# A graph network on one core: the second attention's sums split otherwise between VectorE and TensorE, scatter targets copied by ScalarE, and two runs of 48 gathers limited to four in flight

## The chip, the core and the metric

The kernel runs on one core of one Trainium2 chip. It is written in Bass: each engine (TensorE or PE, VectorE or DVE, ScalarE or ACT, GpSimd or POOL, and SyncE or SP, which issues transfers) runs its own instruction stream, and semaphores are the only order between them. The metric is the device time of one execution in microseconds (us). The kernel before took 3353.75 us, the median of three runs (3352.17 to 3357.39).

## What is computed

A graph of 1250 nodes (768 numbers each) and 20000 edges, sorted by destination, goes through a pre-norm GATv2 block of two attentions (8 heads, then 1 head) and a relational graph encoder with 34 relations and one GCN step. The second attention is what the change is about; in it `heads` is 1 and each edge needs

```
fs = x @ Ws + bs;  fd = x @ Wd + bd
e = leaky_relu(fs[src] + fd[dst], 0.2)        # one row of 768 per edge
logits = sum(e * attn)
m = segment_max(logits, dst)
ex = exp(logits - m[dst]);  denom = segment_sum(ex, dst)
out = segment_sum(ex / denom[dst] * fs[src], dst)
```

The leaky ReLU is split as 0.2·s + 0.8·max(s, 0); the first part is linear and comes ready in column 768 of the projected rows, so the edge work is one add (fs + fd), one `max(·,0)·attn` with a sum along the row, and a weighted sum of rows.

## The kernel before

**Chunks.** The edges are cut into groups of S = 4 edges of one destination; 128 groups, one on each partition, are a chunk. A record (`rec`) names each group's four source rows, its destination, and where its partial sum goes. There are 44 chunks, as 11 turns of a loop over U = 4 buffer slots.

**The stage `attention_single`.** For each chunk:

- SP loads the record (L961), three chunks ahead, once the old record of that slot has been read; one of the reads it waits for is the copy of the scatter target (`to_ok`).
- POOL, two chunks ahead of the arithmetic (`gather_rows`), issues one indirect gather of the destination's `fd` row (`own`, L893) and four of the `fs` rows (`row`, L889), 128 rows of 776 numbers each. Then it issues the scatter of an older chunk's sums (`second_d<-sum`, L942) and copies the scatter target of the chunk out of its record (`to<-rec`, L933), so that the record's slot can be loaded anew.
- DVE adds `own` to rows 0, 1 and 2 (L1392, three instructions, both inputs in SBUF). PE forms the sum of row 3 in PSUM: identity × row, then identity × own, in two halves of 384 columns (L1345 and L1347). DVE then makes four dot products (L1405): `max(sum,0)·attr` with an accumulated sum, for rows 0 to 2 with both tensors in SBUF, for row 3 with the sum in PSUM. Small instructions follow: softmax arguments (L1414 to L1419), relation counts (L1428, L1432), the running denominator (L1440, L1442).
- ACT takes the exponentials (L1325), makes five diagonal matrices of the weights (L1329) and later copies the chunk's sum out of PSUM (L1317). PE multiplies the diagonals with the four rows (L1360) and with the running sum (L1365).

DVE's order in one turn is: arguments of chunk n, counts of n, sums and dots of n+1, denominator of n. PE's order is: pS of n+1, then the products of n.

**Two runs of gathers elsewhere.** In the first stage, which sorts the edges and projects the rows, POOL issues 48 gathers (EARLY) of edge groups one behind the other (L510), then 20 marks; a mark (L222) waits for the mark four before it. In the stage between attention and relations it issues 48 gathers of count rows (L1817). In both runs all gathers raise one semaphore, which is waited for once, at its full count.

## Time and profile before

| | us |
|---|---|
| median of 3 runs | 3353.75 |
| the profiled execution | 3372.56 |
| its span, first to last instruction | 3371.1 |
| PE busy | 2760.3 |
| DVE busy | 2187.0 |
| POOL busy | 1722.6 |
| ACT busy | 1617.7 |

Only 1.5 us of the profiled execution lie outside its span. A share of busy time says little here, because the stages have different limits: the second attention lasts about 410 us of the span, and the long product of the relations (L2263) over 1000.

### The profile page before, as it was taken

Reading aid. Unit: us, or ns where it says so; the run is one execution under the profiler, and the core shown is the slowest. Engines: PE = TensorE matmul, PEld = TensorE weight load, DVE = VectorE, ACT = ScalarE, POOL = GpSimd, SP = SyncE. Lnnn points to the kernel's source line nnn. Section 1 sums busy time; section 2 is a strip of 40 time slices with the busy share of each in tenths; the row PEclk is TensorE's granted clock in tenths of the full one; section 3 lists DMA queues with packets and bytes.
Section 4 is the critical chain, followed back from the end, with each engine's and each line's share of the span. In section 5 each row is a group of like instructions: output and inputs, shape, how many; then the busy total and the mean of one; then the engine's idle time right before and its main releaser. Section 6 shows DMA issues by size and latency. Waiting matters only on the chain. (4 is left out here: it accounts for less than half of the span.)

```text
span 3371.1 us, 53614 instructions
## 1 busy us (share of the span) xinstructions
PE 2760.3 (82%) x11962; PEld 2042.9 (61%) x11985; DVE 2187.0 (65%) x3989; ACT 1617.7 (48%) x5047; POOL 1722.6 (51%) x2089
## 2 busy tenths in 40 slices
PE   5637789888689799995377999999999976676599
PEld 3314445454345455552247999999999973333499
DVE  6503789989666689884365666566566646767554
ACT  0000799999622133331344655656665556767100
POOL 3660556556477588883503444444444436767200
PEclk9859899999889899996698999999999998888799
DMA  4212546555442577775228777777777756667412
GB/s 141 84 18 91 175 151 182 168 170 174 155 120 81 168 230 227 233 231 186 66 91 267 231 245 240 235 237 243 232 244 237 239 129 213 211 218 221 151 62 85
DMA packets 212101, 596.86 MB, mean 177 GB/s; under 512 B 75813, under 2 KB 78905, under 8 KB 211871
## 3 DMA queue, kind: packets, MB, share of 16 engines
q0 software_dynamic: 96256, 380.68, 36.2%
q1 hardware_dynamic: 93487, 163.45, 15.6%
q10 hardware_dynamic: 22304, 52.11, 4.9%
q8 instruction: 22, 0.36, 0.0%
q14 instruction: 32, 0.26, 0.0%
HBM read 491.85 MB, written 161.57 MB: 194 GB/s over the span
## 5 line engine op out<-in xcount | busy, mean ns | idle before, releaser
L2263 PE MATMUL pO<-wh,gT 128*128 128x384 f32 x3264 | 867.9, 340 | 20.8 <-ACT gT L2214 8.3
L2263 PEld LDWEIGHTS pO<-wh,gT 128*128 128x128 f32 x3264 | 593.4, 188 | 26.6 <-issue 13.8
L2263 PE MATMUL pO<-wl,gT 128*128 128x384 f32 x1632 | 546.6, 335 | 0.0
L889 POOL DMA_INDIRECT row<-fs_d,rec x368 | 436.6, 1186 | 113.7 <-issue 112.5
L2279 DVE TENSOR_SCALAR cut<-pT 128x768 int32<-128x768 int32 x137 | 131.0, 956 | 373.1 <-ACT gT L2214 197.2
L1090 ACT ACTIVATE sj<-sj 128x96 f32<-128x96 f32 x1080 | 287.6, 268 | 62.1 <-DVE sj L1202 57.2
L178 PE MATMUL pO<-wt,hT 128*128 128x384 f32 (+1 forms) x720 | 254.6, 512 | 65.8 <-issue 31.4
L2263 PEld LDWEIGHTS pO<-wl,gT 128*128 128x128 f32 x1632 | 307.9, 189 | 0.0
L2214 ACT ACTIVATE gT<-cut 128x256 fp32r<-128x256 f32 x822 | 291.9, 410 | 28.1 <-DVE cut L2282 4.3
L2413 PE MATMUL pR<-row,share 128*128 128x384 f32 x352 | 148.7, 574 | 121.0 <-DMA row<-y_d,rec 39.5
L178 PEld LDWEIGHTS pO<-wt,hT 128*128 128x128 f32 (+1 forms) x720 | 141.9, 199 | 172.9 <-issue 89.8
L889 POOL DMA_INDIRECT row<-y_d,rec x184 | 195.4, 1062 | 92.5 <-issue 47.1
L1128 PE MATMUL pS<-row,ident 128*128 128x384 f32 x368 | 162.7, 525 | 96.1 <-DVE sj L1202 67.0
L222 POOL DMA_INDIRECT marked_d<-marks,recc x160 | 205.6, 1285 | 64.7 <-issue 49.9
L1360 PE MATMUL pA<-row,share 128*128 128x384 f32 x704 | 234.4, 486 | 0.1
L1149 PE MATMUL pA<-row,ident 128*128 128x384 f32 x704 | 234.2, 486 | 0.0
L178 PE MATMUL pO<-settle_wt,hT 128*128 128x384 f32 x480 | 172.4, 519 | 70.2 <-ACT hT L1880 49.8
L2139 POOL DMA_INDIRECT g<-hr_d,gindex x138 | 159.2, 1153 | 126.7 <-POOL keys L2136 74.5
L1090 ACT ACTIVATION_READ_ACCUMULATOR sj<-sj 128x1 f32 x1080 | 202.1, 187 | 8.0 <-issue 8.0
L2203 ACT ACTIVATE sign<-startrow,after 128x1279 bf16<-128x1279 f16 (+1 forms) x139 | 188.4, 1355 | 27.5 <-DMA startrow<-seen_d 26.4
L2292 DVE TENSOR_TENSOR wl<-raw,wh 128x768 fp32r<-128x768 f32 x204 | 195.5, 959 | 7.0
L2133 POOL TENSOR_SCALAR sourcef<-total 128x1 f32<-128x1 f32 x138 | 30.6, 221 | 322.6 <-ACT sign L2203 320.2
(388 smaller groups left out, 5626.6 us busy)
## 6 DMA issues: line engine op xcount, KB each, us to landing
raw<-in_L_gnn_W_rel_dram SPq DMA_DIRECT2D x204, 384.0 KB
startrow<-seen_d ACTq DMA_DIRECT2D x141, 320.0 KB
fs_d<-of SPq DMA_DIRECT2D x18, 388.0 KB
fd_d<-of SPq DMA_DIRECT2D x18, 388.0 KB
row<-fs_d,rec POOLq DMA_INDIRECT x368
ha<-first_d SPq DMA_DIRECT2D x10, 384.0 KB
ha<-second_d SPq DMA_DIRECT2D x10, 384.0 KB
kept_d<-y SPq DMA_DIRECT2D x10, 384.0 KB
```

The lines of the kernel that those rows point to most:

```text
L178: last = pe.matmul(dst[0:rows, q, 0:HALF], rows_t[:, c * P:c * P + rows], w[:, c, lo:up], start=c == 0, stop=c == KC - 1)
L222: pool.indirect_dma_start(marked_d[k], bass.IndirectOffsetOnAxis(ap=keys, axis=0), marks[0:EP], None)\
L889: pool.indirect_dma_start(b["row"][u][:, j, :].bitcast(words), None, table, bass.IndirectOffsetOnAxis(ap=b["rec"][u][:, 2 * j + field:2 * ...
L1090: last = act.activation(of_head, of_head, ACT.Copy, accum_out=dots[off % U][:, j, h:h + 1])
L1128: pe.matmul(pS[j][:, q, 0:HALF], ident[:], row[off % U][:, S // 2 + j, lo:up], start=True, stop=False)
L1149: last = pe.matmul(pA[:, q, 0:HALF], ident[:], row[u][:, j, lo:up], start=j == 0, stop=j == S - 1)
L1360: last = pe.matmul(pA[u % 2][:, q, 0:HALF], share[u % 2][:, 1 + j, :], row[u][:, j, lo:up], start=j == 0, stop=False)
L2139: pool.indirect_dma_start(g[:, b, :], None, hr_d, bass.IndirectOffsetOnAxis(ap=gindex[b][:], axis=0))\
L2203: act.activation(sign[:, 0:COUNT[b]], seen_row[b][:, 0:COUNT[b]], ACT.Sign, bias=half, scale=-1.0, accum_out=total[b][:]).then_inc(total_o ...
L2214: act.activation(gT[:, c].bitcast(F32R), cut[:, :, c * P:(c + 1) * P], ACT.Copy).then_inc(gT_ok.sem, 1)
L2263: last = pe.matmul(pO[:, q, 0:HALF], gT[:, c, half, :].bitcast(F32R), w[:, c, lo:up].bitcast(F32R), start=c == 0 and k == 0, stop=c == KC ...
L2292: dve.tensor_tensor(wl[b][:, c, :].bitcast(F32R), raw[b * KC + c], wh[b][:, c, :], ALU.subtract).then_inc(w_ok.sem, 1)
```

## The change

```
+OPEN = 4
 # first stage, the 48 gathers of L510 (the 48 of L1817 likewise, with crow_in)
+            edges_in2 = sems(st, *[f"edges_in2_{k}" for k in range(OPEN)])
                     for g in range(EARLY):
+                        if g >= OPEN:
+                            pool.wait_ge(edges_in2[g % OPEN], 16 * (g // OPEN))
                         pool.indirect_dma_start(early[:, g, 0:S * 2], None, table_rows, bass.IndirectOffsetOnAxis(
-                            ap=early[:, g, R_ROW:R_ROW + 1], axis=0)).then_inc(edges_in2, 16)
+                            ap=early[:, g, R_ROW:R_ROW + 1], axis=0)).then_inc(edges_in2[g % OPEN], 16)
 # scatter targets: POOL's keep_target is left out in the second attention, ACT does
+        def target_by_act(act, b, i, off):
+            u = off % U
+            rec_wait(act, b, i, off)
+            sum_free(act, b, i, off)
+            act.activation(b["to"][u][:], word(b, u, R_OUT), ACT.Copy).then_inc(b["to_ok"][u], 1)
 # attention_single
+                pW = pb("pW", [P, 2, 512], F32, st)
-                sum_ok = Signal(st, "sum_ok", BY_PE, U, U)
+                sum_ok = Signal(st, "sum_ok", 2, U, U)
                                 keep(i, u - 1)
+                                target_by_act(act, b, i, u)
 # PE
-                            for q, lo, up in HB:
-                                pe.matmul(pS[:, q, 0:HALF], ident[:], row[off % U][:, BY_PE, lo:up],
-                                          start=True, stop=False)
-                                last = pe.matmul(pS[:, q, 0:HALF], ident[:], own[off % U][:, lo:up],
-                                                 start=False, stop=True)
-                            last.then_inc(sum_pe.sem, 1)
+                            pe.matmul(pS[:, 0, 0:HALF], ident[:], row[off % U][:, BY_PE, 0:HALF], start=True, stop=False)
+                            pe.matmul(pS[:, 0, 0:HALF], ident[:], own[off % U][:, 0:HALF], start=False, stop=True)\
+                              .then_inc(sum_pe.sem, 1)
 # DVE
+                        v.mark(dve.tensor_copy(halves(pW), split(attr[:])))
-                            for j in range(BY_PE):
-                                logits.wait(dve, i, off - 1, j + 1)
-                                dve.tensor_tensor(leak[:, j, :], row[off % U][:, j, 0:D], fd[:, 0:D], ALU.add)\
-                                   .then_inc(sum_ok.sem, 1)
+                            logits.wait(dve, i, off - 1)
+                            dve.tensor_tensor(leak[:, 0:BY_PE, :], row[off % U][:, 0:BY_PE, 0:D], over(fd[:, 0:D], 1, [P, BY_PE, D]),
+                                              ALU.add).then_inc(sum_ok.sem, 1)
+                            dve.tensor_tensor(pS[:, 1, 0:HALF], row[off % U][:, BY_PE, HALF:D], fd[:, HALF:D], ALU.add)\
+                               .then_inc(sum_ok.sem, 1)
-                                    ins = dict(out=split(leak[:, j, :]), in0=split(leak[:, j, :]), in1=split(attr[:]))
+                                    ins = dict(out=split(leak[:, j, :]), in0=split(leak[:, j, :]), in1=halves(pW))
```

Five things, then: one DVE instruction of 3 × 768 columns in place of three of 768; row 3's sum half by DVE (SBUF inputs, PSUM output) and half by PE; the attention vector for rows 0 to 2 read from a copy in PSUM (`pW`); the target copy on ACT behind its copy of the sums; and at most four gathers in flight in the two runs of 48.

How DVE's instructions stand in one slot of the loop, from the sums of a chunk to its last dot product. `leak` holds the sums in SBUF, `pS` is the PSUM tile of row 3, `attr` the attention vector in SBUF. Before:

```order
L1392 TENSOR_TENSOR leak<-row_2,own_2 128x768
L239 REGISTER_ALU
L1392 TENSOR_TENSOR leak<-row_2,own_2 128x768
L239 REGISTER_ALU
L1392 TENSOR_TENSOR leak<-row_2,own_2 128x768
L1395 TENSOR_TENSOR lin_2<-row_2,own_2 128x4
L239 ISA
L1405 SCALAR_TENSOR_TENSOR leak,dots_2<-leak,attr 128x768
```

And after (`pW` is the copy of the vector in PSUM):

```order
L1404 TENSOR_TENSOR leak<-row_2,own_2 128x2304
L1406 TENSOR_TENSOR pS<-row_2,own_2 128x384
L1409 TENSOR_TENSOR lin_2<-row_2,own_2 128x4
L240 ISA
L1419 SCALAR_TENSOR_TENSOR leak,dots_2<-leak,pW 128x768 x3
L240 REGISTER_ALU x2
L1419 SCALAR_TENSOR_TENSOR leak,dots_2<-pS,attr 128x768
```

Three adds became one of three times the length, a half-length add that writes PSUM follows it, and three of the four dot products read their second tensor from PSUM. Nothing else changes place on DVE.

How POOL's instructions stand in one slot of the same loop. Before:

```order
L889 DMA row_2<-fs_d,rec_2 128x776 x4
L942 DMA second_d<-sum_2,to_2 2560x912
L933 COPY to_2<-rec_2 128x1
L910 REGISTER_ALU
L239 REGISTER_ALU
L893 DMA own_2<-fd_d,rec_2 128x776
```

And after:

```order
L894 DMA row_2<-fs_d,rec_2 128x776 x4
L954 DMA second_d<-sum_2,to_2 2560x912
L915 REGISTER_ALU
L240 REGISTER_ALU
L898 DMA own_2<-fd_d,rec_2 128x776
```

The copy between the scatter and the next chunk's gathers is gone; the six transfers stay as they were.

## Rows read from the trace of the kernel before

**Rows 1.** Busy time in steady state of the second attention; then a page line, section 5.

```profile
core 0: us, PE busy (x) PEld busy (x) DVE busy (x) ACT busy (x) POOL busy (x), PEclk, DMA share, GB/s
1200.00:1500.00 300.00, 299.60 (x928) 175.60 (x927) 267.32 (x692) 93.52 (x238) 244.55 (x231) 1.00 0.78 231
...
L1360 PE MATMUL pA<-row,share 128*128 128x384 f32 x704 | 234.4, 486 | 0.1
```

**Rows 2.** Groups of instructions, 1200 to 1500 us: busy, mean ns | idle before, releasers.

```profile
L889 POOL DMA_INDIRECT row<-fs_d,rec x132 | 169.9, 1287 | 40.3 <-issue 39.4 <-DMA rec<-groups_d 0.9
L1405 DVE SCALAR_TENSOR_TENSOR leak<-leak,attr 128x768 f32<-128x768 f32 x99 | 89.5, 953 | 0.0
L1392 DVE TENSOR_TENSOR leak<-row,own 128x768 f32<-128x768 f32 x99 | 89.1, 955 | 16.7 <-DMA row<-fs_d,rec 9.3 <-issue 7.3
L1345 PE MATMUL pS<-row,ident 128*128 128x384 f32 x133 | 54.2, 488 | 0.4 <-issue 0.3
L942 POOL DMA_INDIRECT second_d<-sum,to x33 | 35.2, 1067 | 10.1 <-issue 10.1
L893 POOL DMA_INDIRECT own<-fd_d,rec x33 | 32.8, 994 | 5.1 <-issue 5.1
L1405 DVE SCALAR_TENSOR_TENSOR leak<-pS,attr 128x768 f32<-128x768 f32 x33 | 31.5, 954 | 0.6 <-DMA by_dst_d<-recs 0.6
L933 POOL COPY to<-rec 128x1 int32<-128x1 int32 x33 | 7.2, 218 | 0.0
```

**Rows 3.** Waits, 1200 to 1500 us: us in total, times, longest.

```profile
POOL row L889 <- issue: 39.4, 129, 0.3
DVE leak L1392 <- DMA row<-fs_d,rec: 9.3, 14, 1.2
```

**Rows 4.** Timeline of POOL and DVE, 1300 to 1340 us: start, us, instruction, idle before.

```profile
1305.68 2.70 DVE L1392 TENSOR_TENSOR leak<-row,own 128x768 f32<-128x768 f32 x3 [0.83 <-issue]
1305.97 1.48 POOL L889 DMA_INDIRECT row<-fs_d,rec  x1 [0.30 <-issue]
...
1309.50 1.52 POOL L889 DMA_INDIRECT row<-fs_d,rec  x1 [0.30 <-issue]
...
1315.32 2.70 DVE L1392 TENSOR_TENSOR leak<-row,own 128x768 f32<-128x768 f32 x3 [1.19 <-DMA row<-fs_d,rec]
...
1324.29 2.70 DVE L1392 TENSOR_TENSOR leak<-row,own 128x768 f32<-128x768 f32 x3
...
1328.11 1.51 POOL L889 DMA_INDIRECT row<-fs_d,rec  x1 [0.30 <-issue]
...
1333.32 2.69 DVE L1392 TENSOR_TENSOR leak<-row,own 128x768 f32<-128x768 f32 x3 [0.58 <-DMA row<-fs_d,rec]
```

**Rows 5.** Timeline of DVE and POOL in the first stage, 49.5 to 54 us.

```profile
49.84 2.82 DVE L721 TENSOR_TENSOR_SCAN startrow<-keyrow 128x1280 f32<-128x1280 f32 x1
50.77 2.88 POOL L222 DMA_INDIRECT marked_d<-marks,recc  x1 [0.30 <-issue]
52.70 1.49 DVE L722 TENSOR_TENSOR startrow<-startrow,keyrow 128x1280 f32<-128x1280 f32 x1
```

**Rows 6.** Timeline of DVE and POOL where DVE's second tensor is in PSUM.

```profile
2813.15 1.54 DVE L2473 SCALAR_TENSOR_TENSOR sum<-sum,rec,pC 128x1280 int16<-128x1280 int16 x1
...
2813.36 0.94 POOL L889 DMA_INDIRECT row<-y_d,rec  x1 [0.31 <-DVE sum L2468]
```

**Rows 7.** POOL's short transfers by line: duration ns min/median/max, first and last start.

```profile
L222 POOL DMA_INDIRECT marked_d<-marks,recc x160: 1170/1187/2884, 33.2 to 1096.3; - x160
L510 POOL DMA_INDIRECT early<-by_dst_d,early x48: 940/944/1042, 151.6 to 210.4; - x48
L1817 POOL DMA_INDIRECT crow<-rcnt_d,crec x48: 942/946/1680, 1592.4 to 1652.4; - x48
```

**Rows 8.** Two marks in a row; then busy time in two stretches, columns as in rows 1.

```profile
229.96 1.18 POOL L222 DMA_INDIRECT marked_d<-marks,recc  x1 [0.30 <-issue]
231.44 1.18 POOL L222 DMA_INDIRECT marked_d<-marks,recc  x1 [0.30 <-DMA marked_d<-marks,recc]
...
195.00:245.00 50.00, 10.70 (x17) 3.87 (x16) 0.00 (x0) 0.00 (x0) 37.09 (x37) 0.53 0.08 2
1617.00:1655.00 38.00, 0.00 (x0) 0.00 (x0) 0.00 (x0) 0.00 (x0) 28.16 (x31) 0.55 0.13 14
```

More of the change, by code:

```diff
@@ L292, in gnn_kernel @@
             rest_edge = sb("rest_edge", [P, S * 2], I32, st)
-            early_in, edges_in2, masked, edges_out, rest_in, rest_step, rest_out = sems(
-                st, "early_in", "edges_in2", "masked", "edges_out", "rest_in", "rest_step", "rest_out")
+            edges_in2 = sems(st, *[f"edges_in2_{k}" for k in range(OPEN)])
+            early_in, masked, edges_out, rest_in, rest_step, rest_out = sems(
+                st, "early_in", "masked", "edges_out", "rest_in", "rest_step", "rest_out")
             p_index = pb("p_index", [P, 2, 512], F32, st)
@@ L860, in _ @@
                     dve.wait_ge(masked, 1)
-                    dve.wait_ge(edges_in2, 16 * EARLY)
+                    for landed in edges_in2:
+                        dve.wait_ge(landed, 16 * (EARLY // OPEN))
                     dve.tensor_tensor(edges, edges, is_edge[:], ALU.mult).then_inc(masked, 1)
@@ L965, in load_records, with gather_rows @@
                 sp.sem_inc(b["sp_posted"], 1)
-        def gather_rows(pool, b, table, field, own, out_table, readers, done, words=F32):
+        def gather_rows(pool, b, table, field, own, out_table, readers, done, words=F32, targets=True):
             open_sums(pool, b)
@@ L987, in gather_rows @@
                     sums_out(pool, b, i, u - LAG, out_table, done)
-                    keep_target(pool, b, i, u)
+                    if targets:
+                        keep_target(pool, b, i, u)
             for k in range(LAG, 0, -1):
@@ L1304, in _ @@
                     def _(pool):
-                        gather_rows(pool, b, fs_d[0:1 + N], 0, fd_d, second_d, (summed,), (kept, den_ok, counted))
+                        gather_rows(pool, b, fs_d[0:1 + N], 0, fd_d, second_d, (summed,), (kept, den_ok, counted), targets=False)
                     @block.scalar
@@ L1398, in dot @@
                                 if j < BY_PE:
-                                    sum_ok.wait(dve, i, off, j + 1)
-                                    ins = dict(out=split(leak[:, j, :]), in0=split(leak[:, j, :]), in1=split(attr[:]))
+                                    sum_ok.wait(dve, i, off, 1)
+                                    ins = dict(out=split(leak[:, j, :]), in0=split(leak[:, j, :]), in1=halves(pW))
                                 else:
-                                    logits.wait(dve, i, off - 1, j + 1)
+                                    sum_ok.wait(dve, i, off)
                                     sum_pe.wait(dve, i, off)
@@ L1737, in settle_last @@
                     st, "den_in", "rden_ok", "cnt_in", "rcnt_ok", "rcnt_out", "rec_in")
-                crow_in, pool_step, rest_step, rest_out, rest_in = sems(
-                    st, "crow_in", "pool_step", "rest_step", "rest_out", "rest_in")
+                crow_in = sems(st, *[f"crow_in{k}" for k in range(OPEN)])
+                pool_step, rest_step, rest_out, rest_in = sems(
+                    st, "pool_step", "rest_step", "rest_out", "rest_in")
                 rel_const, present_in, summed, joined, seen_ok, seen_out, ntiles_ok, ends_ok, behind_ok, tile_ok = sems(
@@ L1816, in _ @@
                         for g in range(EARLY):
+                            if g >= OPEN:
+                                pool.wait_ge(crow_in[g % OPEN], 16 * (g // OPEN))
                             pool.indirect_dma_start(crow[:, g, :], None, rcnt_d, bass.IndirectOffsetOnAxis(
-                                ap=crec[:, g, R_NODE:R_NODE + 1], axis=0)).then_inc(crow_in, 16)
+                                ap=crec[:, g, R_NODE:R_NODE + 1], axis=0)).then_inc(crow_in[g % OPEN], 16)
                         more = pool.value_load(ctl[0:1, C_REST:C_REST + 1], min_val=1, max_val=MAX_TURNS * U)
@@ L1852, in _ @@
                         pool.sem_inc(posted, 1)
-                        pool.wait_ge(crow_in, 16 * EARLY)
+                        for landed in crow_in:
+                            pool.wait_ge(landed, 16 * (EARLY // OPEN))
                     @block.scalar
```

## The prediction, made before the changed kernel was run

> **What bounds the kernel now.** I first read the busy time of the second attention in steady state [rows 1]. In 300 us PE has 299.6 us of busy time: it looks like the bound. The matmuls are 928, and L942, which comes once a chunk, is there 33 times [rows 2]: 28 matmuls and 9.09 us a chunk, a pitch of 0.323 us, with nothing left. The stage has 704 / 16 = 44 chunks [rows 1].
>
> Then I read the groups of POOL in the same stretch [rows 2]. POOL's busy share is only 244.55 of 300 us, but busy plus the idle time in front of its instructions is 169.9 + 40.3 for the gathers of rows, 35.2 + 10.1 for the scatter, 32.8 + 5.1 for `own` and 7.2 for the copy: 300.6 us. The waits [rows 3] show that the idle part is 129 pauses, none over 0.3 us, put down to "issue": the fixed pause in front of each indirect transfer, not a wait for anybody. So POOL never waits for the other engines, and its stream sets 9.11 us a chunk. DVE, on the other hand, waited 14 times for the rows to land. PE and POOL are both full; DVE is third. From one first add to the next it needs 1333.32 − 1324.29 − 0.58 of waiting = 8.45 us [rows 4].
>
> Last, why POOL's gathers take 1287 ns on average when the 48 alike in the first stage take 944 [rows 2, 7]. In the timeline [rows 4] the gather at 1305.97 takes 1.48 us. It began inside the first of three DVE adds, which ended at 1305.68 + 0.955 = 1306.63, and it ended 0.82 us after that. The mark at 50.77 began inside one DVE scan of 2.82 us and took 2.88 us where the median mark takes 1.187 [rows 5, 7]; it outlasted the scan by 0.99 us. The reading: an indirect transfer that is issued while DVE runs an instruction with two SBUF tensors stands still until that one instruction ends. Where DVE's second tensor is in PSUM, a gather that starts inside DVE's 1.54 us takes 0.94, no stall at all [rows 6].
>
> For this the Trainium skill (SBUF — State Buffer, section "Who interferes with whom") has a rule: a DVE instruction with two SBUF inputs contends with a GpSimd one that reads SBUF, and the pair of ports is held for the whole instruction. The rows agree on GpSimd's side; the reverse, DVE held up by GpSimd, is not seen in them.
>
> **The change part by part.** All sums are in time of the profiled execution (3372.56 us), 19 us above the median of the runs; I add the difference to the median, 3353.75.
>
> PE. Two of four passes each of L1345 and of L1347 go. L1345 is there 133 / 33 = 4 times a chunk and L1347 as often, so 28 matmuls become 24: 24 × 0.323 = 7.76 us a chunk, 1.3 less. PE alone would give 44 × 1.3 = 57 us. This is collected only down to the next full engine.
>
> DVE. One add is 0.955 us [rows 2]; 1280 columns take 1.49 [rows 5], so a column costs (1.49 − 0.955) / 512 = 1.045 ns. The add of 2304 columns is then 0.955 + 1536 × 1.045 ns = 2.56 us, the one of 384 columns 0.55. Adds in a row overlap by about 0.08 us (three take 2.70, not 2.87 [rows 4]). Before: 3 × 0.875 = 2.63 to the next instruction. After: 2.48 + 0.47 = 2.95. DVE's floor becomes 8.45 + 0.32 = 8.77 us. Dots with the vector in PSUM: 954 ns with one PSUM tensor against 953 with none [rows 2], so no change. That the half add writes PSUM is not in the trace; between 0.47 and, if it cost as much as a whole add, 0.87 us, I take 0.47. The 0.4 more would put DVE at 9.2, which is no more than POOL takes below.
>
> POOL. Four things. (a) The copy goes, 0.22 us, but `own` then has the full pause of 0.30 in front of it in place of 5.1 / 33 = 0.155: net 0.07. (b) The stalls of now, 4 × (1.287 − 0.944) = 1.37 us a chunk, go: those in the dots because their vector is now in PSUM, those in the adds because there are no three short ones. POOL without stalls: 9.11 − 0.07 − 1.37 = 7.67. (c) One new stall comes. The long add runs 2.56 us. POOL starts something every 1.25 us (0.944 + 0.30), so some issue must fall inside it. If it starts s after the add, it ends 0.82 us after the add's end instead of 0.944 after its own start: a stall of 2.56 − s − 0.125 = 2.43 − s us, with s between 0 and 1.25. (d) Where s lies: POOL's last gather of a chunk ends at 1311.02 and DVE's add of that chunk starts at 1315.32; or 1329.62 and 1333.32 [rows 4]. That is 3.7 to 4.3 us, and POOL's stream behind a last gather is 0.30 + 1.07 + 0.30 + 0.99 + 0.30 + 0.94 + 0.30 = 4.2 us to the start of the second row gather. With 3.7, s is 0.5 and the stall 1.9; just below 4.2 it is 2.4; at 4.3 the next gather is hit, s = 1.15 and the stall 1.3. The bounds are 1.2 and 2.4; I take 1.9, from the 3.7, since the last three row gathers will follow each other more closely than now and one of the two cases must keep hitting the second gather. POOL: 7.67 + 1.9 = 9.57 us a chunk (8.87 to 10.1).
>
> The half add behind the long one stalls nobody: the released transfer runs 0.82 us and pauses 0.30, and by then it is over.
>
> Sum for the stage: POOL stays the fullest, 9.57 against 9.11, so 44 × 0.46 = +20 us (−11 to +43). DVE will wait for rows more, and PE too: they have 0.8 and 1.8 us of slack a chunk.
>
> ACT. A 128x1 copy a chunk, 0.2 us, on an engine busy 93.5 of 300 us [rows 1]; it is placed behind the copy of the sums. Queued behind it is only the next exponential, which is not due for several us. SP waits for it with the next record, three chunks ahead, and POOL waited for records for 0.9 us in 300 [rows 2]. Nothing, at most the 0.9 doubled.
>
> The copy of the vector to PSUM is one instruction of 0.95 us before the loop, while the first rows are under way. Nothing.
>
> The two throttled runs. A new wait stands in front of 44 of 48 gathers. The gather four before was issued 4 × 1.25 = 5.0 us earlier; a chunk's last gather, 128 rows of 776 numbers behind four others, had landed 3.7 us after its issue ended [rows 4]. With an issue of 0.944 us that would be 4.65 us after its start, and the gathers of the two runs carry a few numbers a row. The marks already wait like this and stay at a pitch of 1.48, with the same 0.30 in front [rows 8]. So the wait is met when it is reached: 0 us, and if one in four were late by 0.3 us, 44 × 0.3 / 4 = 3 us for each run.
>
> Result: 3353.75 + 20 = 3374, less some 2 us for the first chunks, where POOL's lead of two chunks is still being used up: 3372 us.
>
> **The rivals.**
>
> The long add is no lock (faster). If POOL gets in between the three rows of the long add, as it now does between three adds, its stall is some 0.5 us and DVE's floor is the bound: 8.77 against 9.09, 44 × 0.32 = −14 us, 3340. For it: PE is relieved, the dots no longer hold POOL. Against: one scan of 2.82 us held one mark for its whole rest [rows 5].
>
> The phases fall well (no change). The add starts just after the second gather has started: stall 1.2 to 1.4, POOL 8.9 to 9.1, −8 to 0 us, 3350. For it: the 4.3 of one chunk. Against: the 3.7.
>
> The throttle ends a standstill (faster). While POOL runs its 48 gathers the rest of the chip stands almost still: from 1617 to 1655 us PE, DVE and ACT have no instruction at all, from 195 to 245 DVE and ACT none and PE 17 [rows 8]. If that came from gathers being in flight without limit, four at a time would free up to 38 + 50 us: with the +18 above, between 3284 and 3350, say 3310. For it: the standstills lie on these two runs and end with POOL's stream. Against: from 211 us on POOL is issuing marks, which are limited to four already, and the standstill goes on to 245; and by my count fewer than four are in flight anyway.
>
> The Trainium skill (Runtime: NRT & Kernel Launch, section "Instruction fetch mechanics") says that a taken branch out of the loaded window forces a fetch before execution goes on. Such a fetch would be a matter of one transfer, not of 38 us, and no row here shows one; by it the throttle would change nothing.
>
> The half add is dear (slower). If writing PSUM costs DVE 0.87, and the phases give the worst stall of 2.4 in every chunk, POOL is at 10.1: +43 us, 3397. It decides once the adds start within 0.1 us of POOL's second gather.
>
> **How the numbers follow.** The stall of 1.6 to 2.4 us in most chunks: 0.5, time 3360 to 3397, my forecast 3372. Phases fall well: 0.16. No lock: 0.12. The throttle ends the standstill, in whole or part: 0.18. The rest, among it other stages moved by a shifted program: 0.04. 0.2% (7 us) is about what a measurement of this kernel tells from no change. Faster by more: 0.12 + 0.18 + a quarter of 0.16 and half of the rest = 0.36. Within: 0.15. Slower: 0.49. Range for 8 in 10: from 3318, which takes in part of the relief by the throttle, to 3394. The forecast's own range is 3358 to 3394.
>
> **What would show it.** Right: POOL's row gathers show one of 2.5 to 3.2 us a chunk and the others 0.95, with the start of the long one inside the add of 2304 columns; POOL still has no pause over 0.3 us; PE's busy time falls to about 81% of the stretch; a chunk takes 9.4 to 9.8 us; the two standstills last as long as before. Wrong: no gather over 1.6 us; or DVE without any wait for rows at 8.8 us a chunk; or PE, DVE and ACT at work between 1617 and 1655.

## The result, and the profile after

The changed kernel takes 3370.08 us, the median of eight runs (3353.06 to 3385.87); the kernel before, run beside it, 3353.22 (eight runs, 3341.77 to 3360.68). The ratio is 1.006, 95% interval 1.004 to 1.0081: 17 us slower by the medians and 20 by the ratio, where 18 were forecast. The profiled execution is 3385.87 us, its span 3384.4.

The stage from the first `own` gather of the second attention to its last scatter of sums took 420.7 us before and takes 439.6, 18.9 more. Ahead of that stage the profiled execution lost nothing (it was 7.6 us shorter, mostly in the first attention, which the change does not touch), behind it 2.0 us came on top: 18.9 − 7.6 + 2.0 = 13.3, the difference of the two spans. Such differences outside the stage are noise: over all the executions that were profiled here, the first `own` gather of the second attention starts between 1108 and 1125 us. The stage itself repeats well. Where its code is that of the kernel before it took 420.7, 419.3 (with the throttle alone) and 420.3 us (with one gather in flight).

The busy time of the same 300 us of steady state, columns as in [rows 1]:

```profile
1200.00:1500.00 300.00, 254.26 (x748) 140.58 (x749) 264.56 (x623) 92.06 (x263) 242.70 (x189) 0.99 0.72 219
```

PE has given up its full 300 us; POOL is as busy as before (242.70 against 244.55) although it does fewer chunks (31 scatters in the stretch, not 33). The groups and waits of that stretch, to be laid beside [rows 2, 3]:

```profile
L894 POOL DMA_INDIRECT row<-fs_d,rec x126 | 182.7, 1450 | 38.4 <-issue 37.2 <-DMA rec<-groups_d 0.6 <-PE pA L1372 0.6
L1404 DVE TENSOR_TENSOR leak<-row,own 128x2304 f32<-128x2304 f32 x32 | 81.9, 2559 | 20.7 <-DMA row<-fs_d,rec 15.7 <-issue 4.9
L1406 DVE TENSOR_TENSOR pS<-row,own 128x384 f32<-128x384 f32 x31 | 17.3, 559 | 0.0
L954 POOL DMA_INDIRECT second_d<-sum,to x31 | 31.4, 1012 | 9.4 <-issue 9.4
L1359 PE MATMUL pS<-row,ident 128*128 128x384 f32 x64 | 29.3, 540 | 42.0 <-DMA row<-fs_d,rec 37.2 <-issue 4.7
L945 ACT ACTIVATE to<-rec 128x1 int32<-128x1 int32 x31 | 5.9, 190 | 0.0
```

```profile
POOL row L894 <- issue: 37.2, 122, 0.3
DVE leak L1404 <- DMA row<-fs_d,rec: 15.7, 20, 1.2
PE pS L1359 <- DMA row<-fs_d,rec: 37.2, 25, 2.1
```

POOL's row gathers now average 1450 ns against 1287, and POOL still pauses for nothing but its fixed 0.3 us; DVE and PE wait for rows, 20 and 25 times. From one scatter to the next a chunk takes 9.605 us against 9.103. Taken by their place in the chunk the four gathers average 953, 2846, 1037 and 952 ns (before: 967, 1237, 1444, 1510). The timeline shows why it is the second:

```profile
1297.17 0.95 POOL L894 DMA_INDIRECT row<-fs_d,rec  x1 [0.30 <-issue]
1297.79 2.56 DVE L1404 TENSOR_TENSOR leak<-row,own 128x2304 f32<-128x2304 f32 x1 [0.66 <-DMA row<-fs_d,rec]
1298.42 2.75 POOL L894 DMA_INDIRECT row<-fs_d,rec  x1 [0.30 <-issue]
...
1301.48 0.95 POOL L894 DMA_INDIRECT row<-fs_d,rec  x1 [0.31 <-issue]
...
1307.57 2.56 DVE L1404 TENSOR_TENSOR leak<-row,own 128x2304 f32<-128x2304 f32 x1 [1.02 <-DMA row<-fs_d,rec]
1307.85 3.10 POOL L894 DMA_INDIRECT row<-fs_d,rec  x1 [0.30 <-issue]
```

Each second gather shown began inside the long add. The add of 1297.79 ends at 1300.35; the gather that began inside it, at 1298.42, ends at 1301.17, 0.82 us later. With s = 0.63 the stall by 2.43 − s is 1.80, and 0.944 + 1.80 = 2.74 us; the row has 2.75. The next has s = 0.28, so 3.09, and the row 3.10. The mean gather of 2846 ns is a mean stall of 1.90 us, the value that the sum took.

In a few chunks the add catches the third gather, because the second just slips in, having started together with the add:

```profile
1442.69 2.59 DVE L1404 TENSOR_TENSOR leak<-row,own 128x2304 f32<-128x2304 f32 x1 [0.57 <-issue]
1442.69 0.96 POOL L894 DMA_INDIRECT row<-fs_d,rec  x1 [0.30 <-issue]
...
1443.95 2.15 POOL L894 DMA_INDIRECT row<-fs_d,rec  x1 [0.30 <-issue]
```

The gather of 1442.69 begins 5 ns into the add and takes its 0.96 us, and this add takes 2.59 us, where those that find a gather well under way, or none, take 2.55 to 2.56. Over all kernels here gathers that began up to 0.04 us into such an add slipped in in some cases, later ones never.

The throttled run in the first stage keeps its pace: 48 gathers, first start to last start 58.8 us as in [rows 7]; and so does the other (60.0 us as before).

```profile
L514 POOL DMA_INDIRECT early<-by_dst_d,early x48: 940/944/1042, 150.3 to 209.1; - x48
L1834 POOL DMA_INDIRECT crow<-rcnt_d,crec x48: 944/944/1680, 1603.9 to 1663.9; - x48
```

The standstills stay too. The one between attention and relations lies 11 us later, as its gathers do, so the prediction's sign of being wrong, "PE, DVE and ACT at work between 1617 and 1655", is met by the letter (PE is busy for 9.91 us of them) and says nothing; the same stretch 11 us on is empty but for one DVE instruction:

```profile
1628.00:1666.00 38.00, 0.00 (x0) 0.00 (x0) 0.96 (x1) 0.00 (x0) 28.65 (x31) 0.54 0.11 16
```

### The profile page after: what moved, and what is told of

Same layout as the page of the kernel before. It is cut to its first block and busy times, and to the rows that moved or that the text cites. A ratio compares the mean times of both kernels' runs of the same rounds, so it can differ in the third digit from the quotient of the medians.

```text
span 3384.4 us, 53081 instructions
## 1 busy us (share of the span) xinstructions
PE 2718.5 (80%) x11804; PEld 2005.1 (59%) x11805; DVE 2202.1 (65%) x3945; ACT 1620.9 (48%) x5091; POOL 1733.7 (51%) x2045
## 5 line engine op out<-in xcount | busy, mean ns | idle before, releaser
L2281 PEld LDWEIGHTS pO<-wh,gT 128*128 128x128 f32 x3264 | 593.4, 188 | 25.0 <-ACT gT L2232 12.4
L894 POOL DMA_INDIRECT row<-fs_d,rec x368 | 466.4, 1267 | 113.6 <-issue 112.1
L223 POOL DMA_INDIRECT marked_d<-marks,recc x160 | 205.9, 1287 | 64.4 <-issue 51.1
L179 PE MATMUL pO<-settle_wt,hT 128*128 128x384 f32 x480 | 172.4, 519 | 72.0 <-ACT hT L1898 49.5
L1372 PEld LDWEIGHTS pA<-row,share 128*128 128x128 f32 x704 | 134.7, 193 | 104.1 <-issue 14.2
```

Of the source, the lines that this page charges most:

```text
L179: last = pe.matmul(dst[0:rows, q, 0:HALF], rows_t[:, c * P:c * P + rows], w[:, c, lo:up], start=c == 0, stop=c == KC - 1)
L223: pool.indirect_dma_start(marked_d[k], bass.IndirectOffsetOnAxis(ap=keys, axis=0), marks[0:EP], None)\
L894: pool.indirect_dma_start(b["row"][u][:, j, :].bitcast(words), None, table, bass.IndirectOffsetOnAxis(ap=b["rec"][u][:, 2 * j + field:2 * ...
L1372: last = pe.matmul(pA[u % 2][:, q, 0:HALF], share[u % 2][:, 1 + j, :], row[u][:, j, lo:up], start=j == 0, stop=False)
L2281: last = pe.matmul(pO[:, q, 0:HALF], gT[:, c, half, :].bitcast(F32R), w[:, c, lo:up].bitcast(F32R), start=c == 0 and k == 0, stop=c == KC ...
```

## The experiments

Twelve kernels ran. Eleven were timed beside the kernel before on the same chip (12 executions each, but 5 of the long add alone and 9 of the long add with the vector). They ran in three groups, each on a chip of its own, so it is the ratios that can be compared between kernels, not the medians. Ratios are to the kernel before; "chunk" is the mean time from one scatter of sums to the next between 1200 and 1500 us, "stage" is as above, both from the one profiled execution of each.

| kernel | median us | ratio, 95% interval | chunk | stage | four row gathers, mean ns |
|---|---|---|---|---|---|
| before | (first profile) | | 9.10 | 420.7 | 967 1237 1444 1510 |
| changed | 3370.1 | 1.006 (1.004 to 1.0081) | 9.61 | 439.6 | 953 2846 1037 952 |
| throttle only | 3351.5 | 0.9993 (0.997 to 1.0016) | 9.08 | 419.3 | 970 1218 1449 1511 |
| long add only | 3392.6 | 1.0126 (1.009 to 1.0162) | 10.16 | 466.6 | 952 2576 1653 1036 |
| vector in PSUM only | 3354.2 | 1.0013 (0.9992 to 1.0034) | 9.11 | 429.1 | 1025 978 947 970 |
| half add only | 3350.5 | 1.0006 (0.9988 to 1.0024) | 9.02 | 415.5 | 949 1049 1388 1124 |
| target copy on ACT only | 3347.9 | 0.9989 (0.9971 to 1.0007) | 9.18 | 423.6 | 1015 1338 1458 1500 |
| long add and vector | 3371.9 | 1.0059 (1.0037 to 1.0081) | 9.47 | 436.3 | 949 2636 1066 945 |
| changed, short adds | 3357.0 | 1.0029 (1.0001 to 1.0058) | 9.10 | 422.2 | 1232 1005 952 953 |
| changed, two rows + one | 3354.0 | 1.0005 (0.9986 to 1.0024) | 9.22 | 422.9 | 1196 1023 961 956 |
| changed, half add first | 3346.4 | 0.9978 (0.996 to 0.9997) | 9.19 | 422.7 | 953 1024 2060 1333 |
| short adds, split at 512 | 3346.6 | 0.9994 (0.997 to 1.0018) | 8.99 | 419.0 | 1028 956 1016 1203 |
| three of these together | 3344.9 | 0.9992 (0.9973 to 1.0011) | 8.91 | 411.3 | 956 976 1720 1180 |

### The parts by themselves

**The long add alone**, on the kernel before:

```
-                            for j in range(BY_PE):
-                                logits.wait(dve, i, off - 1, j + 1)
-                                dve.tensor_tensor(leak[:, j, :], row[off % U][:, j, 0:D], fd[:, 0:D], ALU.add)\
+                            logits.wait(dve, i, off - 1)
+                            dve.tensor_tensor(leak[:, 0:BY_PE, :], row[off % U][:, 0:BY_PE, 0:D], over(fd[:, 0:D], 1, [P, BY_PE, D]),
```

> The kernel before with the three adds made one, and nothing else: PE adds the whole of row 3, the vector stays in SBUF. Theory: one gather a chunk is held 1.9 us by the add and the next 0.6 by a dot product; POOL 9.11 - 1.37 + 2.5 = 10.2 us a chunk, 44 x 1.1 = 50 us more, 3395 to 3410. Rival A (the add's length does not matter): PE stays the bound at 9.05 to 9.1, 3350 to 3355.

The slowest of all: a chunk of 10.16 us as expected, and 3392.6, 2 us under the range expected. Its timeline:

```profile
1300.90 2.56 DVE L1391 TENSOR_TENSOR leak<-row,own 128x2304 f32<-128x2304 f32 x1 [1.76 <-DMA row<-fs_d,rec]
1301.58 2.70 POOL L889 DMA_INDIRECT row<-fs_d,rec  x1 [0.30 <-issue]
...
1304.38 0.95 DVE L1404 SCALAR_TENSOR_TENSOR leak<-leak,attr 128x768 f32<-128x768 f32 x1
1304.58 1.57 POOL L889 DMA_INDIRECT row<-fs_d,rec  x1 [0.30 <-issue]
```

Two gathers are caught, one by the add and one by a dot product with both tensors in SBUF. Each ends 0.82 us after the DVE instruction it began in: 1300.90 + 2.56 + 0.82 = 1304.28, and 1304.38 + 0.95 + 0.82 = 1306.15. DVE itself takes 2.56 and 0.95 us whether a gather stands or not.

**The vector in PSUM alone** (`pW` and its use, nothing else):

```
+                pW = pb("pW", [P, 2, 512], F32, st)
+                        v.mark(dve.tensor_copy(halves(pW), split(attr[:])))
-                                    ins = dict(out=split(leak[:, j, :]), in0=split(leak[:, j, :]), in1=split(attr[:]))
+                                    ins = dict(out=split(leak[:, j, :]), in0=split(leak[:, j, :]), in1=halves(pW))
```

> The kernel before with the vector of three dot products read from PSUM, and nothing else. Theory: the gathers that start in the dots take 0.95 us, those in the three adds 1.0 to 1.6; POOL needs some 8.5 us a chunk, so PE with its 28 matmuls is the bound at 9.05, POOL waits for it; 0 to 3 us less than before, 3349 to 3354. Rival (the dots do not hold POOL, the second input's place changes nothing): gathers of 1.4 to 1.5 us stay, 9.1 a chunk, 3353.

The row gathers fall to 947 to 1025 ns, so 1.24 us of stalls a chunk have left them, and the time does not change beyond its uncertainty (though the stage of the profiled execution is 8.4 us longer). About 0.5 us of it came back on other instructions of POOL, the `own` gather and the copy of the target; the other 0.7 us went into a new wait, for PE:

```profile
1200.00:1500.00 300.00, 298.79 (x926) 175.32 (x925) 265.10 (x688) 94.01 (x239) 220.82 (x231) 1.00 0.73 230
```

```profile
POOL row L889 <- issue: 40.5, 129, 1.5
POOL own L893 <- PE pA L1361: 19.7, 10, 2.2
```

```profile
L893 POOL DMA_INDIRECT own<-fd_d,rec x33 | 39.2, 1187 | 28.0 <-PE pA L1361 19.7 <-remote 4.3 <-issue 4.0
L933 POOL COPY to<-rec 128x1 int32<-128x1 int32 x33 | 18.4, 559 | 0.0
```

PE is busy 298.79 of 300 us: with 28 matmuls it is the bound at 9.1 us, just behind POOL. That is why this relief alone does not show.

**Both together** (the two edits above, on the kernel before):

> The kernel before with two parts, the long add and the vector in PSUM; row 3 stays all on TensorE, the target copy on POOL. The long add by itself gave 10.16 us a chunk, with two stalls (about 1.6 and 0.7 us by the mean gather durations). My theory: with the vector in PSUM the stalls in the dots go and one of 1.9 us is left; POOL is 9.11 - 1.37 + 1.9 = 9.6 us a chunk, so 3373 (3365 to 3380), the same as the whole change, and nothing of the change's loss comes from the half add, the target or the throttle. Rival, the half add and the relief of TensorE bring the changed kernel part of its distance to the long add alone: then this one is at 9.8 to 10.1, 3382 to 3392.

Ratio 1.0059, and the whole change has 1.006. The same dot product with its vector in PSUM holds nobody: the third row below starts inside the dot of the second and takes 0.94 us.

```profile
1297.64 2.72 POOL L889 DMA_INDIRECT row<-fs_d,rec  x1 [0.30 <-issue]
...
1300.45 0.95 DVE L1406 SCALAR_TENSOR_TENSOR leak<-leak,pW 128x768 f32<-128x768 f32 x1
1300.66 0.94 POOL L889 DMA_INDIRECT row<-fs_d,rec  x1 [0.30 <-issue]
```

So these two edits carry the loss, one making it (+42 us alone, by its ratio) and the other taking about half of it back (+20 us together; in the stage 15.6 of the whole change's 18.9 us). The chunk is 9.47 where 9.6 was expected; the forecast of 3373 was met.

**The half add alone**:

```
-                            for q, lo, up in HB:
-                                pe.matmul(pS[:, q, 0:HALF], ident[:], row[off % U][:, BY_PE, lo:up],
+                            pe.matmul(pS[:, 0, 0:HALF], ident[:], row[off % U][:, BY_PE, 0:HALF], start=True, stop=False)
+                            dve.tensor_tensor(pS[:, 1, 0:HALF], row[off % U][:, BY_PE, HALF:D], fd[:, HALF:D], ALU.add)\
```

> The kernel before with only row 3's split: 384 columns of its sum by VectorE into PSUM. TensorE goes from 28 x 0.323 = 9.05 to 7.76 us, VectorE's floor from 8.45 to 8.92. My theory: POOL with its stalls in adds and dots is still the bound, 9.0 to 9.2 us a chunk, so no change, 3353 (3346 to 3360). Rival, one more VectorE instruction with two SBUF tensors catches one more gather: +0.3 us a chunk, 3366. Rival, TensorE was the bound after all: 8.9 us a chunk, 3345.

No change, 1.0006. In its profile the chunk is 9.02. PE is relieved, and the two engines left are both full. POOL still has no pause over 0.3 us: three of its four row gathers are shorter than before, but its scatter takes 1479 ns instead of 1067, for the half add catches it. DVE no longer waits for rows; from one `lin` add to the next its chunks take 8.80 us three times and 9.48 at each turn of the loop, 8.97 in the mean. Which of the two bounds this kernel can't be told.

**The target copy alone** (`keep_target` left out on POOL, `target_by_act` added on ACT):

> The kernel before with only the copy of the scatter target moved from GpSimd to ScalarE. GpSimd's stream gets 0.07 us a chunk shorter (0.22 less the fuller pause), to 9.04; TensorE has 9.05. My theory: 0 to 3 us less, 3351, not to be told from no change. Rival, SyncE now gets the record's slot late, because ScalarE copies it behind its copy of the sums: waits for records show up in front of the row gathers and the time is 3356 to 3366.

No change, 0.9989. POOL's stream stays full at 9.18 us a chunk: the rest of its pause in front of `own` (0.31 us instead of 0.155) and row gathers that are a little longer use up what the copy gave back.

**The throttle alone** (`OPEN = 4` and its semaphores):

> The kernel before with nothing but the two runs of 48 gathers limited to four in flight. Theory: the wait is met when it is reached; the pace of the gathers stays at 1.25 us, both standstills stay, 3350 to 3356. Rival B (the limit costs or moves something): 3360 to 3370. Rival C (gathers in flight without limit cause the standstills): 38 to 88 us less, 3265 to 3315.

No change, 0.9993; the idle stretches stay (PE has no instruction from 228 to 248 us and from 1605 to 1652). The rival "the throttle ends a standstill" falls. To see what the standstill is, the same kernel ran with one gather in flight, `OPEN = 1`:

> The kernel before with only the throttle, and that at one gather in flight instead of four. With four the wait was met when it was reached and nothing changed. With one, each gather waits for the one before to land: a pitch of 2.5 to 4 us instead of 1.25, so each run of 48 takes 120 to 190 us instead of 60. If the standstill of the other engines comes from POOL's stream being busy with gathers or from transfers in flight, it thins out now, since POOL idles more than half of the time; the whole kernel is then 20 to 120 us longer, as far as the runs are on the path. If it comes from something else that the other engines wait for in data, it keeps its work and just lasts as long as the runs, 120 to 260 us longer in all.

The runs took 133 and 149 us in place of 60 and 61. The kernel was executed once, in 3348.26 us, which is within the spread of the kernel before (3341.77 to 3360.68). The busy time of one stretch in each run of gathers, of the kernel before, then of this one:

```profile
155.00:205.00 50.00, 25.36 (x71) 13.82 (x69) 6.64 (x40) 1.93 (x3) 37.81 (x41) 0.75 0.17 36
1600.00:1650.00 50.00, 15.27 (x42) 8.32 (x40) 7.92 (x17) 8.31 (x10) 38.12 (x40) 0.60 0.21 45
```

```profile
155.00:205.00 50.00, 46.83 (x156) 27.86 (x155) 18.26 (x104) 5.86 (x9) 14.98 (x16) 1.00 0.31 97
1600.00:1650.00 50.00, 41.31 (x133) 23.97 (x131) 36.00 (x75) 32.69 (x41) 15.68 (x15) 0.90 0.43 132
```

With the gathers 2.8 and 3.1 us apart PE works 46.83 of 50 us, not 25.36, and 41.31, not 15.27. The standstill belongs to POOL's stream of gathers at full pace, then; whether to their issue or to their transfers this run can't tell, since both are slower in it. Little of it is time lost, because what PE does meanwhile it would otherwise do right after: the engines idle later instead, from 246 to 284 and 294 to 336 us, until POOL's longer run and the marks behind it are over. The first attention's row gathers start at 343.1 us instead of 332.8, so the first run costs about 10 us at that place; for the second no loss shows. The expectation of 20 to 120 us more is not borne out by the one execution. The same rows settle how many were in flight at all: one lands at most 2.8 us after it starts, and at a pitch of 1.25 that is 2.2 at a time (2.5 for the count rows), so a limit of four is never met.

### The length of the long add, and its place

**Three short adds** in the changed kernel (three instructions of one row each again, with `BY_PE + 1` signals; the one wait in front of them stays):

> The changed kernel with its one add of 2304 columns taken apart again into three of 768; all else of the change stays. Theory (one long DVE instruction with two SBUF tensors holds POOL's gather for its whole rest): no gather over 1.7 us, POOL at 7.67 + two stalls of some 0.5 = 8.7 us a chunk, DVE's floor 8.45 + 0.47 = 8.92 becomes the bound; 8.9 to 9.1 us a chunk, 0 to 8 us less than the kernel before, 3345 to 3353. Rival A (the loss comes from the half add into PSUM or from the copy on ACT, not from the length of the add): 9.6 us a chunk as in the changed kernel, 3370.

3357.0, ratio 1.0029: some 10 us by the ratios, and in the stage 17.4 of 18.9 us, are back, since POOL's long stall is gone; but the kernel is not faster than before, which I had expected it to be. POOL now waits for PE's products (18.2 us, 7 times, in front of `own`), and DVE waits for nobody for long: its longest wait in 300 us is 1.5, for itself.

```profile
DVE ge L1443 <- DVE ex L1434: 5.3, 9, 1.5
DVE lg L1429 <- issue: 3.9, 9, 0.4
```

From one `lin` add to the next its chunks take 8.73 or 8.74 us (8.92 was expected), but about 9.5 at the turn of the loop, every fourth, and now and then 10. So 9.10 is no longer POOL's figure but DVE's with what the turn adds; what that is stays open.

One thing that neither the prediction nor any experiment took apart: where PE is relieved and the chunk stays short, TensorE's granted clock (the third number from the end) drops below full in the same 300 us. Here and with the half add alone:

```profile
1200.00:1500.00 300.00, 268.46 (x791) 151.98 (x789) 278.38 (x726) 94.92 (x268) 213.20 (x199) 0.97 0.74 231
1200.00:1500.00 300.00, 275.34 (x800) 155.65 (x799) 283.46 (x740) 94.46 (x240) 244.15 (x234) 0.95 0.77 233
```

It is 1.00 before, where PE is hardly ever idle, 0.99 in the changed kernel and 0.96 with two rows and one. The drops are stretches of 3.4 or 6.8 us at the lower of the two levels, 1.2 instead of 2.4 GHz. With the half add alone, where the share is lowest, no chunk is longer than 9.48 us, so they cost nothing there; whether they lengthen chunks in the other kernels is not shown.

**Two rows and one row**:

```
-                            dve.tensor_tensor(leak[:, 0:BY_PE, :], row[off % U][:, 0:BY_PE, 0:D], over(fd[:, 0:D], 1, [P, BY_PE, D]),
-                                              ALU.add).then_inc(sum_ok.sem, 1)
+                            dve.tensor_tensor(leak[:, 0:2, :], row[off % U][:, 0:2, 0:D], over(fd[:, 0:D], 1, [P, 2, D]),
+                                              ALU.add).then_inc(sum_ok.sem, 1)
+                            dve.tensor_tensor(leak[:, 2, :], row[off % U][:, 2, 0:D], fd[:, 0:D], ALU.add)\
+                               .then_inc(sum_ok.sem, 1)
```

> The changed kernel with the long add of three rows cut into one of two rows (1536 columns, 1.76 us by the 1.045 ns a column) and one of one row (0.96 us). My theory: the gather caught by the first stands 1.76 - 0.63 - 0.125 = 1.0 us and is let in when that add ends; its last 0.82 us and the pause of 0.30 cover the second add, which catches nobody. POOL needs 7.67 + 1.0 = 8.7 us, below DVE; with DVE or PE's feedback as the bound a chunk takes 9.0 to 9.15 us as with three short adds, and the time is about 3357 (3348 to 3364). Rival, what costs is not the stall but the wait of the first dot and of TensorE for a sum that comes all at once: two rows at once would keep most of it, 9.4 us a chunk, 3365. Rival, DVE's own work bounds: one instruction fewer than three adds, 3350.

3354.0, ratio 1.0005, inside the 3348 to 3364 expected; the chunk, 9.22 us, is longer than the 9.0 to 9.15 expected, for two chunks of the stretch take 13.7 and 12.4 us, of which no experiment gives the cause. The caught gather is let in between the two adds, although the second follows at once:

```profile
1303.13 1.75 DVE L1404 TENSOR_TENSOR leak<-row,own 128x1536 f32<-128x1536 f32 x1
1303.20 2.52 POOL L894 DMA_INDIRECT row<-fs_d,rec  x1 [0.30 <-issue]
...
1304.80 0.95 DVE L1406 TENSOR_TENSOR leak<-row,own 128x768 f32<-128x768 f32 x1
```

1303.13 + 1.75 + 0.82 = 1305.70, and the gather ends at 1305.72, inside the second add. The hold is one instruction's, not a series'.

**The same instructions in another order**: the half add and the small `lin` add ahead of the long one, which is moved down unchanged.

```
+                            dve.tensor_tensor(pS[:, 1, 0:HALF], row[off % U][:, BY_PE, HALF:D], fd[:, HALF:D], ALU.add)\
+                               .then_inc(sum_ok.sem, 1)
...
                             dve.tensor_tensor(leak[:, 0:BY_PE, :], row[off % U][:, 0:BY_PE, 0:D], over(fd[:, 0:D], 1, [P, BY_PE, D]),
...
-                                    sum_ok.wait(dve, i, off, 1)
+                                    sum_ok.wait(dve, i, off)
```

> The changed kernel with the same instructions in another order: the half add and the small lin add stand ahead of the long add, so that the long add starts some 0.6 us later against POOL's stream; the dots of rows 0 to 2 wait for it as before. My theory (one stall of 2.43 - s us, s from the start of the long add to the gather that is caught): in the changed kernel s is about 0.63 at the second row gather; started 0.6 us later the long add begins as that gather begins or just behind it, so the third one is caught instead, with s 0.8 to 1.2 and a stall of 1.2 to 1.6. POOL is then at 7.67 + 1.4 = 9.1 us a chunk, the long gather is the third of the four in most chunks, and the time is about 3352 (3345 to 3362). Rival, only the length of the long add counts: the place in the stream makes no difference, 9.6 us a chunk, 3370. Rival, the phase is not held and the second gather is still caught with s near 0.1 to 0.3: stall 2.2, 9.9 us a chunk, 3380.

3346.4, ratio 0.9978 (0.996 to 0.9997). The same work, by the ratios 27 us less than the changed kernel, and in the stage 16.9 us less: the place alone takes away nearly all of the loss. As expected the third gather is caught instead of the second (2060 ns against 2846 at its place), with a larger s:

```profile
1297.56 0.57 DVE L1404 TENSOR_TENSOR pS<-row,own 128x384 f32<-128x384 f32 x1 [0.22 <-DMA row<-fs_d,rec]
1297.80 1.15 POOL L894 DMA_INDIRECT row<-fs_d,rec  x1 [0.30 <-issue]
...
1306.90 0.97 POOL L894 DMA_INDIRECT row<-fs_d,rec  x1 [0.30 <-issue]
1306.97 0.56 DVE L1404 TENSOR_TENSOR pS<-row,own 128x384 f32<-128x384 f32 x1
1307.51 2.55 DVE L1409 TENSOR_TENSOR leak<-row,own 128x2304 f32<-128x2304 f32 x1
1308.18 2.71 POOL L894 DMA_INDIRECT row<-fs_d,rec  x1 [0.31 <-issue]
...
1316.30 0.96 POOL L894 DMA_INDIRECT row<-fs_d,rec  x1 [0.30 <-issue]
1316.43 2.55 DVE L1409 TENSOR_TENSOR leak<-row,own 128x2304 f32<-128x2304 f32 x1
1317.57 2.24 POOL L894 DMA_INDIRECT row<-fs_d,rec  x1 [0.31 <-issue]
```

At 1316.43 s is 1.14, a stall of 1.29 and a gather of 2.24 us. POOL's chunk falls from 9.61 to 9.19 us, as expected (9.1). Its stream is still full, with no pause over 0.3 us; DVE hardly waits for rows any more (1.1 us in 300, against 15.7), PE does (17.6 us). The stage, 422.7 us, is 2.0 us longer than before, so that the ratio lies below 1 is not explained by the attention.

**Row 3 split at column 512**, with three short adds: TensorE makes 512 columns of the sum in one half of the PSUM tile, VectorE 256 in the other.

```
-                            pe.matmul(pS[:, 0, 0:HALF], ident[:], row[off % U][:, BY_PE, 0:HALF], start=True, stop=False)
+                            pe.matmul(pS[:, 0, :], ident[:], row[off % U][:, BY_PE, 0:512], start=True, stop=False)
-                            dve.tensor_tensor(pS[:, 1, 0:HALF], row[off % U][:, BY_PE, HALF:D], fd[:, HALF:D], ALU.add)\
+                            dve.tensor_tensor(pS[:, 1, 0:D - 512], row[off % U][:, BY_PE, 512:D], fd[:, 512:D], ALU.add)\
```

> The changed kernel with three short adds, and row 3 split at column 512 instead of 384: TensorE makes 512 columns of the sum in one bank, DVE 256 in the other, and the dot reads 768 columns in one piece. DVE's add gets 128 columns x 1.045 ns = 0.13 us shorter, TensorE goes from 24 x 0.323 = 7.76 to about 8.0 us. My theory, that with three short adds DVE is the bound (8.73 us in its quiet chunks): 0.13 us x 44 = 6 us less than with the split at 384 (3357), so 3351 (3342 to 3358). Rival, the bound there is the round trip between DVE, ACT and TensorE once a turn and not DVE's work: no difference, 3357. Rival, TensorE and DVE in neighbouring banks of a tile that is read in one piece cost something: 3365.

DVE's quiet chunks are 8.60 to 8.66 us, 0.1 less, as reckoned; the time, 3346.6, ratio 0.9994, is inside the range. The interval overlaps that of the split at 384, so a gain over that one is not shown.

**All of it together**: split at 512, the small adds first, then two rows, then one.

> The three things that helped, together: the changed kernel with row 3 split at column 512 (256 columns on VectorE), that quarter-size add and the lin add ahead of the big one, and the big one cut into two rows and one row. My theory: the add of two rows begins some 0.4 us later than a long add at the front would, so it catches the second row gather with a small s or the third with a large one; the stall is 1.76 - s - 0.125, 0.8 to 1.5 us, and POOL at 7.67 + 1.2 = 8.9 us stays at or below the others. VectorE's quiet chunks are 8.6 to 8.65 us, about 9.3 once a turn, so 8.85 a chunk: 3343 (3336 to 3350). Rival, what POOL loses to the two-row add matters again: 9.1 a chunk, 3352. Rival, the gains are one and the same (VectorE no longer waits for rows) and don't add up: 3347.

3344.9, ratio 0.9992. Its profile has the shortest chunk (8.91) and stage (411.3, 9.4 less than before), but its interval takes in 1, so that it is faster than the kernel before is not shown. Of all versions only the reordered one has an interval that lies below 1, by 0.0003, and one in twelve may do so by chance; whether one of the two is the better can't be told from these runs.

## Why the prediction was right

**What bounds the kernel: right for the changed kernel, not settled for the one before.** In the changed kernel POOL pauses for nobody and the others wait for its rows; the long add alone gives it the same stalls and more, and the chunk follows, to 10.16 us. In the kernel before, POOL and PE are full together [rows 1, 2]. The vector alone took POOL's stalls away and the pace stayed at 9.11, now PE's; the half add alone took PE's work away and it stayed at 9.02, with POOL and DVE both full.

**The lock: right, in its three points.** It holds for the rest of one DVE instruction (gathers end 0.82 us after adds of 2304, 1536 and 768 columns and after a dot); it needs both tensors in SBUF (1.57 against 0.94 us for a gather inside the same dot with its vector in SBUF or in PSUM); a short instruction behind the long one catches nobody further. What the prediction's formula lacks is the edge: a gather that starts just as the add does (5 and 30 ns into it in the two cases of the changed kernel) can slip in, and then the next one is held. The rule that the prediction drew from the Trainium skill (SBUF — State Buffer, section "Who interferes with whom"), a pair of ports held for the whole instruction, fits the two-row add, which lets the gather in though another add follows at once. The same section says that whichever of the two starts first keeps the other out. In the other direction the traces show only tens of ns: the long add at 1297.79 began 0.62 us into a gather and took 2.56 us, no more than the others' mean of 2559 ns, but the two adds of the changed kernel whose gather slipped in at their start (5 and 30 ns into them) took 2.59 and 2.62 us.

**The size of the stall: right, in part by luck.** Taken 1.9, measured 1.90 on the second gather. The value hung on s = 0.5, read from one chunk of two (3.7 us from POOL's last gather to the add; the other, at 4.3, would have given 1.3). The mean of that distance turned out to be 3.82 us before and 3.76 after, so the choice held, but two chunks could not show it; s spreads from 0.08 to 1.27 us. And two small errors cancel: all four row gathers together stall 2.01 us a chunk, not 1.9, and POOL without them needs 9.605 − 2.01 = 7.59 us, not 7.67, since the prediction left out the little stalls of `own` and the scatter (994 and 1067 ns before, 975 and 1012 after). A chunk was put at 9.57.

**PE: right in its sign, its size off.** Forecast 24 × 0.323 = 7.76 us a chunk and 81% busy; measured 254.26 us over 300 / 9.605 = 31.2 chunks, 8.14 us and 85%. The pitch of 0.323 holds for matmuls back to back (sixteen in 5.32 us at 1299.27 in the changed kernel, 15 × 0.323 + 0.486 = 5.33); a matmul behind a wait is counted with its full 0.486 and more (L1359 has 540 ns in the mean). PE was off the path, so nothing hung on it.

**DVE: a little less than forecast.** The half add was put at 0.55 and takes 0.559, the long one at 2.56 and takes 2.559; the price of writing PSUM, left open up to 0.87, is nothing that shows. DVE's shortest chunk in the changed kernel is 8.66 us, where the floor was put at 8.77. The floor left out what a turn of the loop adds, 0.7 us in every fourth chunk (9.48 against 8.80 with the half add alone).

**ACT, the copy of the vector, the throttle: nothing, as forecast.** The 190 ns copy on ACT costs nothing: SP waits for it (46.5 us in 300, where it waited 119.3 us for POOL's copy before), but POOL waits for records for only 0.6 us. The count of fewer than four gathers in flight was right (2.2).

**The sum.** 44 × 0.46 − 2 = 18 us was forecast for the stage and 18.9 was there. Rivals: "no lock" is refuted by every timeline above; "the phases fall well" did not happen in the changed kernel but is just what the reordered one does; the throttle did nothing; the worst case of 2.4 us came in single chunks (gathers of up to 3304 ns), not in the mean. Of the standstill the prediction had asked only whether the throttle ends it; that the work would then only move, as it does with one gather in flight, was not foreseen, and the rival's 38 + 50 us were probably too much on that ground too.

## What to carry to other kernels

Before you join short VectorE instructions with two SBUF operands into a long one, look at what GpSimd issues meanwhile: the join saves VectorE some 0.14 us here and can cost GpSimd nearly the length of the whole instruction (2.36 of 2.56 us at worst), and how much it costs hangs on where in GpSimd's stream the instruction starts. Move the second operand to PSUM where you can (here that is shown for the dot products), and if you must have the long instruction, put the short ones that need not come later in front of it and see which transfer it catches. Where two engines are both full, a relief of one shows nothing until the other is relieved too, so judge parts of a change in pairs.

## What the runs showed of the hardware

- A gather that starts inside a VectorE instruction with two SBUF inputs ends 0.82 us after that instruction, whether it is 0.95, 1.75 or 2.56 us long; a gather needs 0.95 us undisturbed. One that starts together with the instruction, up to 0.04 us into it, can slip in, and then the instruction takes 0.03 to 0.07 us longer (2.59 and 2.62 us instead of 2.56 in the changed kernel). A gather that is further along, or one that is held, does not slow VectorE.
- A VectorE add of SBUF tensors that writes PSUM takes 559 ns for 384 columns and some 425 ns for 256 (427 and 424 in the two kernels that have it), and a gather that began inside such an add in the reordered kernel ended 0.82 us behind it as well (1297.56 + 0.57 + 0.82 = 1298.95, and the gather of 1297.80 lasts 1.15).
- An indirect gather of a few numbers a row lands at most 2.8 us after its issue begins (133 us for 48 one by one).
- While GpSimd issues gathers every 1.25 us in straight-line code, TensorE, VectorE and ScalarE do less than half of the work that they do when the gathers come every 2.8 us (25.36 against 46.83 us busy in 50). In the attention, where gathers come at the same distance but in a loop, TensorE is busy throughout. What it is that the others lack then stays open.
